# A memory layer and eight experts in one kernel: new wave order, stacked gated-bias product, last expert by pairs of tiles

## The reference, cut to what matters

```
x  = x + ln(memory(ln(x)))          # layer 1
x  = x + ln(experts(ln(x)))         # layer 2

memory(x):
  k, q, v = x@Wk+bk, x@Wq+bq, x@Wv+bv;  alr = 0.1*sigmoid(x@Wlr+blr)
  h1 = k + silu(k@W1+b1);  pred = h1 + silu(h1@W2+b2)
  loss = sum(alr * mean((pred - v)**2))      # gradients of W1, b1, W2, b2 over all tokens
  p_new = p*(1-1e-4) - 0.01*g/(sqrt(g*g)+1e-8)     # one Adam step of each
  return the same two layers with the new W1, b1, W2, b2, applied to q

experts(x):
  z = ln(x)*g + b;  p = softmax(z@rW + rb);  w = the two largest p, over their sum, 0 elsewhere
  y = sum over e of w[e] * (gelu(z@W1[e]+b1[e]) @ W2[e] + b2[e])    # 8 experts, hidden width 256
  return x + y
```

## Time and profile before

| | us |
|---|---|
| median of three runs | 206.26 |
| profiled execution | 204.86 |
| its span | 203.1 |
| PE busy | 178.0 (88%) |
| DVE busy | 145.4 (72%) |
| ACT busy | 99.1 (49%) |
| POOL busy | 22.1 (11%) |

### The profile page before, as it was taken

One profiled execution on the slowest core, in us unless ns is written; L12 is line 12 of the kernel. 1 busy time (PEld: TensorE's weight loads), 2 busy tenths in 40 slices (PEclk: granted clock), 3 DMA queues, 4 the chain that ended last, 5 costly groups with the idle time before them and its releaser, 6 DMA issues.

```text
span 203.1 us, 3196 instructions
## 1 busy us (share of the span) xinstructions
PE 178.0 (88%) x1089; PEld 140.8 (69%) x1089; DVE 145.4 (72%) x564; ACT 99.1 (49%) x150; POOL 22.1 (11%) x30
## 2 busy tenths in 40 slices
PE   7388988897988796999999999999999999999930
PEld 7334454465644484879999699988799897889920
DVE  0987695879685799979348977668976656475474
ACT  2157682946444309934567326384355495334200
POOL 1440000000000140032000131001211000010010
PEclk9999999999999999999999999999999999999996
DMA  5970000000000000000000000100000100001001
GB/s 153 342 233 4 0 0 3 0 0 0 0 3 2 0 2 0 3 0 0 3 0 2 0 3 0 52 3 0 2 0 3 52 0 3 2 2 52 3 0 52
DMA packets 3232, 4.96 MB, mean 24 GB/s; under 512 B 240, under 2 KB 1552, under 8 KB 3216
## 3 DMA queue, kind: packets, MB, share of 16 engines
q1 hardware_dynamic: 3216, 4.76, 7.2%
HBM read 3.71 MB, written 1.05 MB: 23 GB/s over the span
## 4 chain that ended last, share of the span: by engine, by line
PE 69%; DVE 17%; ACT 7%; issue 3%; DMA 2%; POOL 0%; POOLq 0%; DVEq 0%; ACTq 0%
PE bank L330 65%; DVE stats L737 3%; PE bank L338 2%; DMA x_tok<-in_x_dram 2%; ACT sig L580 2%; DVE xnT L1020 2%; ACT nsig L587 2%; DVE mv L740 1%; DVE s L870 1%; DVE s L878 1%; DVE xnT L874 1%; DVE vT L881 1%; ACT s L580 1%; ACT alrT L580 1%; ACT kT L576 1%
## 5 line engine op out<-in xcount | busy, mean ns | idle before, releaser
L1020 DVE SCALAR_TENSOR_TENSOR xnT<-bank,w_tok,xnT 128x128 f32<-128x128 f32 x128 | 36.0, 344 | 27.7 <-PE bank L330 27.3
L297 POOL TENSOR_TENSOR rstd<-vpe,minus_half 128x4 f32<-128x4 f32 (+1 forms) x21 | 20.7, 995 | 175.5 <-DVE vpe L745 162.0
L330 PE MATMUL bank<-z_hi,fW_hi 128*128 128x512 f32 x64 | 27.8, 435 | 1.5 <-DVE z_lo L915 1.5
L330 PE MATMUL bank<-z_lo,fW_hi 128*128 128x512 f32 x64 | 25.2, 394 | 0.0
L330 PE MATMUL bank<-z_hi,fW_lo 128*128 128x512 f32 x64 | 25.0, 390 | 0.0
L330 PEld LDWEIGHTS bank<-fW_sb,sig 128*128 128x128 f32 x192 | 22.8, 192 | 2.2 <-ACT h1T L686 1.5
L330 PE MATMUL bank<-fW_sb,sig 128*128 128x128 f32 x192 | 23.4, 276 | 0.0
L686 ACT ACTIVATE sig<-bank,early_sb 128x512 f32<-128x512 f32 x24 | 16.2, 688 | 13.8 <-PE bank L330 13.7
L686 ACT ACTIVATE k_tok<-bank,early_sb 128x512 f32<-128x512 f32 x20 | 13.5, 688 | 15.4 <-PE bank L330 15.3
L330 PEld LDWEIGHTS bank<-fW_sb,k_tok 128*128 128x128 f32 x160 | 19.3, 191 | 1.5 <-ACT sig L686 0.8
L330 PEld LDWEIGHTS bank<-fW_sb,h1T 128*128 128x128 f32 x160 | 19.3, 191 | 1.5 <-ACT k_tok L686 0.8
(11 more groups left out here) (129 smaller groups left out, 270.4 us busy)
## 6 DMA issues: line engine op xcount, KB each, us to landing
x_tok<-in_x_dram SPq DMA_DIRECT2D x4, 256.0 KB, 4.4
fW_raw<-in_fW_dram SPq DMA_DIRECT2D x1, 1024.0 KB, 9.2
out_dram<-xn_tok SPq DMA_DIRECT2D x3, 256.0 KB, 2.5
early_sb<-in_early_dram SPq DMA_DIRECT2D x1, 268.0 KB, 4.1
late_sb<-in_late_dram SPq DMA_DIRECT2D x1, 264.0 KB, 4.8
out_dram<-xn_tok SPq DMA_DIRECT2D x2, 128.0 KB, 2.0
b_diag<-in_late_dram SPq DMA_DIRECT2D x4, 4.0 KB
fW_sb<-in_fW_dram SPq DMA_DIRECT2D x1, 0.5 KB, 11.7
```

Of the source, the lines that this page charges most:

```text
L297: pool.tensor_tensor(rstd[:, ln, where], vpe[:, ln, where], minus_half[:, 0:where.stop - where.start], ALU.pow).then_inc(rstd_ready[ln], 1)
L330: return pe.matmul(out_, lhsT, rhs, start=start, stop=stop)
L1020: last = dve.scalar_tensor_tensor(out=y_tok[:, t, :], in0=bank[Y_BANK[m % len(Y_BANK)]][:, i * P:(i + 1) * P], scalar=w_tok[:, t, e:e + 1] ...
```

## The change

- `WAVE` and `LAG` are new. 1 - sigmoid is a step of its own (`n1`, `n2`), behind `h1` and behind `k`. `alr` now belongs to block w, not w + 1, and comes earlier; it leaves the prologue. `fw` begins a wave earlier (its first piece is in ACT's prologue) and DVE's `fw1_low(w)` is in wave w, the last piece behind the loop.
- Adam: the biases' sum comes first, and their chain is interleaved with W2's, not with W1's.
- Bias term: DVE writes four copies of the weights next to each other (high part twice, low part twice; 128 columns), in two more instructions at the end of `route`; they are transposed into 128 rows. `b2_diag` has 128 rows (high, low, high, low), so that one fp32r product gives the sum. It is filled by 16 small transfers, and POOL makes its rounded parts in three instructions of 512 columns, behind `rsqrt(L1, 0)`.
- Last expert: `output(31)` writes its first two tiles to bank 4 and the others to bank 7, and signals after each pair. DVE adds the first pair, takes its statistics, adds the second, takes its statistics, and then does the two `y_norm`.
- ACT subtracts the residual's mean from `x1_tok` (four instructions per block, slots 4, 12, 20, 28), so `y_norm` loses two small linked instructions.

```diff
-        WAVE = ["dh1", "dz2", "z2", "h1", "z1", "dz1", "gw2", "k", "gw1", "v", "alr", "x", "kp", "fw"]
-        LAG = {"dh1": -1, "dz2": -1, "z2": 0, "h1": 0, "z1": 1, "dz1": -1, "gw2": -1, "k": 0, "gw1": -1,
-               "v": 1, "alr": 1, "x": 3, "kp": 2, "fw": 0}
+        WAVE = ["dh1", "dz2", "z2", "h1", "n2", "z1", "alr", "gw2", "dz1", "v", "gw1", "k", "n1", "kp", "x", "fw"]
+        LAG = {"dh1": -1, "dz2": -1, "z2": 0, "h1": 0, "n2": 0, "z1": 1, "alr": 0, "gw2": -1, "dz1": -1,
+               "v": 1, "gw1": -1, "k": 0, "n1": 1, "kp": 2, "x": 3, "fw": 1}
...
-            for t in range(TB):
-                sp.dma_start(b2_diag[t * E:(t + 1) * E, t * H:(t + 1) * H],
+            for first in range(0, P, E):
+                t = first // E % TB
+                sp.dma_start(b2_raw[first:first + E, t * H:(t + 1) * H],
                              late[0:E, b2_first:b2_first + b2_width]).then_inc(b2_in, 16)
...
             rsqrt(L1, 0)
+            pool.wait_ge(b2_in, 16 * P // E)
+            pool.tensor_scalar(b2_diag[:], b2_raw[:], 1.0, 0.0, ALU.mult, ALU.add).then_inc(b2_high, 1)
+            pool.wait_ge(b2_high, 1)
+            for i, first in enumerate((TE, 3 * TE)):
+                rows = slice(first, first + TE)
+                pool.tensor_tensor(b2_diag[rows, :], b2_raw[rows, :], b2_diag[rows, :].bitcast(F32),
+                                   ALU.subtract).then_inc(b2_ready, 1)
+                pool.wait_ge(b2_ready, i + 1)
...
             def w_transpose(b):
-                pe.wait_ge(w_ready, b + 1)
+                pe.wait_ge(w_low, b + 1)
                 pe.wait_ge(zhi_done, b + 1)
-                pe.transpose(bank[7][0:TB * E, 0:P], w_tok[:, TB * b:TB * b + TB, :].rearrange("p t e -> p (t e)"),
-                             ident[:]).then_inc(w_tr, 1)
+                pe.transpose(bank[7][:, 0:P], w_parts[:, b, :].bitcast(F32), ident[:]).then_inc(w_tr, 1)
...
                 for i in range(TB):
+                    if m == STEPS - 1:
+                        into = bank[LAST_BANK[i // HALF]]
+                        if i == HALF:
+                            last.then_inc(y_mm, 1)
...
+            def centre_residual(b):
+                act.wait_ge(init_done, b + 1)
+                act.wait_ge(shift_ready, b + 1)
+                for t in tiles(b):
+                    last = act.activation(x1_tok[:, t, :], x1_tok[:, t, :], ACT.Identity, bias=neg_shift[:, t:t + 1])
+                last.then_inc(centred, 1)
...
-                if w:
-                    fw1_low(w - 1)
+                if w < NB - 1:
+                    fw1_low(w)
                 if w < NB:
                     layer2(w)
+            fw1_low(NB - 1)
             dve.wait_ge(late_in, 16)
             dve.wait_ge(gw2_mm, 1)
-            run(adam(w2n[:], w2_sb, bank[0][:, 0:P], adam_tmp[:, 0, :], adam_tmp[:, 1, :], w2n_ready))
             dve.wait_ge(dz1_done, NB)
             run(link(dve.tensor_reduce(gbs[:], gb[:], AX_X, ALU.add)))
+            run(adam(w2n[:], w2_sb, bank[0][:, 0:P], adam_tmp[:, 0, :], adam_tmp[:, 1, :], w2n_ready),
+                adam(bn[:], cols[:, B1:B1 + 2], gbs[:], gb_tmp[:], gb[:, 0, 0:2], bn_ready))
             dve.wait_ge(w2n_ready, 1)
             dve.wait_ge(gw1_mm, 1)
-            run(adam(w1n[:], w1_sb, bank[4][:, 0:P], adam_tmp[:, 0, :], adam_tmp[:, 1, :], w1n_ready),
-                adam(bn[:], cols[:, B1:B1 + 2], gbs[:], gb_tmp[:], gb[:, 0, 0:2], bn_ready))
+            run(adam(w1n[:], w1_sb, bank[4][:, 0:P], adam_tmp[:, 0, :], adam_tmp[:, 1, :], w1n_ready))
...
                 dve.tensor_tensor(tok(w_tok, b), p, first, ALU.mult).then_inc(w_ready, 1)
+                yield
+                dve.wait_ge(w_ready, b + 1)
+                weight = tok(w_tok, b).rearrange("p t e -> p (t e)").unsqueeze(1).to_broadcast([P, 2, TE])
+                parts = w_parts[:, b, :].rearrange("p (i c) -> p i c", c=TE)
+                dve.tensor_scalar(parts[:, 0:2, :], weight, 1.0, None, ALU.mult).then_inc(w_high, 1)
+                yield
+                dve.wait_ge(w_high, b + 1)
+                dve.tensor_tensor(parts[:, 2:4, :], weight, parts[:, 0:2, :].bitcast(F32),
+                                  ALU.subtract).then_inc(w_low, 1)
...
-            run(y_stats(NB - 1), y_stats(NB))
-            run(y_norm(NB - 1), y_norm(NB))
+            add_last_expert(0)
+            run(y_stats(NB - 1))
+            add_last_expert(1)
+            run(y_stats(NB))
+            run(y_norm(NB - 1))
+            run(y_norm(NB))
```

More of the change, by code:

```diff
@@ L141, in memory_and_experts @@
         rstd = sb("rstd", [P, 5, T])
-        shift = sb("shift", [P, 2, T])
+        neg_shift = sb("neg_shift", [P, T])
         minus_half = sb("minus_half", [P, TB])
@@ L156, in memory_and_experts @@
             "zeroed", "ident_ready", "half_ready", "table_ready", "ramp_ready"))
-        b2_zeroed, b2_in, fw_hi_done, fw_lo_done = (sem(n) for n in (
-            "b2_zeroed", "b2_in", "fw_hi_done", "fw_lo_done"))
+        b2_zeroed, b2_in, b2_high, b2_ready, fw_hi_done, fw_lo_done = (sem(n) for n in (
+            "b2_zeroed", "b2_in", "b2_high", "b2_ready", "fw_hi_done", "fw_lo_done"))
         dve_step = sem("dve_step")
@@ L225, in memory_and_experts @@
         H_BANK, Y_BANK, B2_BANK = (0, 1, 5), (6, 2), 3
+        LAST_BANK = (4, 7)
+        HALF = TB // 2
         AHEAD = 2
@@ L306, in _ @@
                       allow_small_or_imprecise_dtypes=True).then_inc(ramp_ready, 1)
-            pool.memset(b2_diag[:], 0.0).then_inc(b2_zeroed, 1)
+            pool.memset(b2_raw[:], 0.0).then_inc(b2_zeroed, 1)
             rsqrt(LR_, 0)
@@ L419, in _ @@
             k_product(1)
-            alr_product(0)
             feature_major_x(2)
@@ L667, in wT_out @@
                 act.wait_ge(w_tr, b + 1)
-                copy(wT[:, b * P:(b + 1) * P], bank[7][0:TB * E, 0:P], wT_ready)
+                copy(wT[:, b * P:(b + 1) * P], bank[7][:, 0:P], wT_ready)
             rsig1_out(0)
@@ L694, in _ @@
                     wT_out(0)
+                if slot >= 0 and slot % E == CENTRE:
+                    centre_residual(slot // E)
                 if due(Z_TR, slot):
@@ L897, in residual @@
                 last.then_inc(x1_ready, 1)
-                dve.tensor_tensor(shift[:, 0, span(b)], mv[:, LR_, span(b), 0], rstd[:, LR_, span(b)],
-                                  ALU.mult).then_inc(shift_ready, 1)
+                dve.scalar_tensor_tensor(out=neg_shift[:, span(b)], in0=mv[:, LR_, span(b), 0], scalar=-1.0,
+                                         in1=rstd[:, LR_, span(b)], op0=ALU.mult,
+                                         op1=ALU.mult).then_inc(shift_ready, 1)
                 yield
@@ L1024, in add_expert, with add_last_expert @@
                 last.then_inc(acc_done, 1)
+            def add_last_expert(half):
+                dve.wait_ge(y_mm, STEPS + half)
+                dve.wait_ge(acc_done, STEPS - 1)
+                for i in range(half * HALF, half * HALF + HALF):
+                    t = T - TB + i
+                    last = dve.scalar_tensor_tensor(out=y_tok[:, t, :],
+                                                    in0=bank[LAST_BANK[half]][:, i * P:(i + 1) * P],
+                                                    scalar=w_tok[:, t, E - 1:E], in1=y_tok[:, t, :],
+                                                    op0=ALU.mult, op1=ALU.add)
+                last.then_inc(acc_done, 1)
             def y_stats(q):
                 first, count = PARTS[q]
-                dve.wait_ge(acc_done, (first // TB + 1) * E)
+                dve.wait_ge(acc_done, (first // TB + 1) * E + (1 if q == NB else 0))
                 yield from statistics(LY, range(first, first + count), lambda i, t: y_tok[:, t, :])
@@ L1037, in y_norm @@
                 dve.wait_ge(rstd_ready[LY], q + 1)
[L1038 to L1041, removed]
-                yield from link(dve.tensor_tensor(shift[:, 1, where], shift[:, 1, where],
-                                                  shift[:, 0, where], ALU.subtract))
+                dve.wait_ge(centred, where.start // TB + 1)
                 for t in range(where.start, where.stop):
-                    last = dve.tensor_scalar(y_tok[:, t, :], y_tok[:, t, :], rstd[:, LY, t:t + 1],
-                                             shift[:, 1, t:t + 1], ALU.mult, ALU.add)
+                    last = dve.tensor_scalar(y_tok[:, t, :], y_tok[:, t, :], mv[:, LY, t, 0:1],
+                                             rstd[:, LY, t:t + 1], ALU.subtract, ALU.mult)
                 yield from link(last)
@@ L1068, in _ @@
                         start_sum(slot // E)
-                    add_expert(slot)
+                    if slot < STEPS - 1:
+                        add_expert(slot)
                 if due(NORM_R, slot):
```

29 lines of the change are left out of this document (18 added, 11 removed).

## The result

The changed kernel takes 196.88 us (median of four runs, 196.28 to 197.03) against 206.24 us (the three runs of before and a fourth, 204.58); the ratio is 0.958 with a 95% interval of 0.954 to 0.962. The ratio leaves slow runs out and is not the quotient of the two medians, which is 0.955. The forecast was 198.6 us, with a range of 196.4 to 201.2. The profiled executions differ by 8.1 us (204.86 and 196.74), their spans by 8.5. The remaining 1.2 us of the 9.4 are in the medians: that of before lies 1.4 above its profile, as was said, that of the changed kernel 0.1 above its own. The sum is therefore judged by the spans. Part of this level goes with PE's clock: of the runs of the kernel before that stand beside the experiments, 33 enter the ratios and have their span and mean granted clock on record.

A forecast was written before the change was run, and what follows sets the result against it. PE was taken to bound the experts' part, step order the first stage. First stage -5.9, Adam 0, POOL +1.2, experts -1.2, end -1.75 make -7.65; from 206.26 that gives 198.6 us, range 196.4 to 201.2.

The forecast's parts named there:

- rival 1: Retrieval, before the first hidden product: POOL's b2 instructions do not disturb DVE; -8.85, 197.4 us; chance 25%.
- a walk 0.6 better than mine: First stage: the step-by-step timing of the waves, which gave -5.9, improved by 0.6 for the range's low end.
- First stage, -5.9: Waves up to dh1(3): with the waits gone PE bounds a full wave at 8.9 us; dh1(3) at 46.2, not 52.13.
- Adam, 0: Adam's new order changes nothing, since its end stays covered by PE's work, with 0.8 us of cover left.
- POOL, +1.2: Retrieval: one of POOL's three b2 instructions, at 1.1 us, stands fully in DVE's way; +1.2 us.
- Bias term, -0.85: Experts' part: one fp32r product for the bias term gains 0.85 us per block, -2.55 for blocks 1 to 3.
- The two waits of +0.5: At w_transpose of blocks 1 and 2, PE waits 0.5 us longer each for the end of the routing.
- Block 0, +0.27: At output(2), PE waits for expert 0's sum, 0.5 us later on DVE; +0.27 instead of -0.85.
- End, -1.75: After the last product: last expert by pairs, fewer small linked steps; additions end 1.75 us earlier, last transfer moves with them.
- the third: First stage: the waves do not close up, only the waits visible in the rows go (-3.3); 201.2 us; chance 10%.
- the fourth: POOL's elementwise work costs what its rsqrt does, 80 us per instruction; slower than before; chance 2%.
- the second: The lock decides every meeting for POOL, holding DVE's two-input instructions twice; +2.1 instead of +1.2, 199.5 us; chance 20%.

The follow-up runs named there:

- e1: The kernel before with the new wave order alone (1 - sigmoid split off, alr moved, W1 pieces a wave earlier): 199.9 us, ratio 0.971.
- e5: The kernel before in its old wave order, with only the 1 - sigmoid steps moved behind h1 and behind k: 203.14 us, ratio 0.990.
- e6: The kernel before with the new order of the other steps, 1 - sigmoid still directly behind its sigmoid: 200.45 us, ratio 0.976.
- e4: The changed kernel with Adam in the old order (biases beside W1): 196.75 us, ratio 0.961.
- e9: The changed kernel with POOL's three b2 instructions behind a wait for the new W1: 196.16 us, ratio 0.957.
- e10: The changed kernel with memsets in place of POOL's two subtractions, low part of b2 left out: 195.79 us in a single run.
- e7: The changed kernel with POOL's three b2 instructions moved ahead of the first rsqrt of the retrieval: 196.62 us, ratio 0.957.
- e2: The kernel before with the stacked gated-bias product alone (its POOL, PE and DVE parts): 204.73 us, ratio 0.998.
- e3: The kernel before with the last expert by pairs of tiles alone, y_norm as before: 204.86 us, ratio 0.997.
- e11: e9 with the weights' transpose of blocks 1 to 3 half a slot later, between two hidden products: 194.65 us, ratio 0.951.
- e12: e11 with block 0's two weight instructions behind norm_r(1), its transpose behind output(0), and ten clock-keeping transposes: 194.9 us, ratio 0.948.

## Why the prediction was right

The forecast of 198.6 us was too high by 1.7, and the mechanism is to be judged by the stretches, not by the total: 196.88 us is nearer to rival 1's 197.4 than to the forecast, yet POOL's rows refute rival 1. It also lies only 0.5 above the low end of the range, and that end rested on a walk 0.6 better than mine, beyond the -6.2 that the prediction itself gave as about the end. That the sum comes within 0.9 of the spans' -8.5 is in part luck, as two terms below show.

- **First stage, -5.9:** -6.06 once the load's 0.36 is taken out. That PE bounds a full wave at 8.9 was right (8.99). e1 shows the part alone; e5 and e6 show that inside the waves the order does it. My weighing of ACT's chain against the queue ahead of `dh1` was left open in the prediction: either alone shortens the waves (1.6 and 3.6 us), but they do not add (3.6 together).
- **Adam, 0:** right (e4).
- **POOL, +1.2:** right in cause (e9, e10) and, up to the first hidden product, in size (+1.15). It was the forecast's least certain term, taken from one stretched POOL row. It was split otherwise than I had it: not one hold, but one of 1.0 and one of 0.3. And the forecast carried it in full to `output(2)`, where only 0.84 of it arrives (e9 against e4).
- **Bias term, -0.85:** too small. It is 1.02: 0.92 up to the output, so the 0.07 that I had allowed for unprefetched weights was not there, and 0.10 behind it. Three times 0.17 are 0.5 of the 0.6 us that the stretch to the last product came out better than forecast. The two waits of +0.5 were right (0.53); block 3's +0.1 was 0.
- **Block 0, +0.27:** +0.55 was measured, but by another mechanism: PE was late by its clock, and DVE's sum was there in time. Where the clock was full and POOL out of the way (e7, e9) it is +0.35, with the predicted wait of PE for DVE (1.24 in e9). From `dh1(3)` to `output(2)` the measured +1.70 is thus 0.84 of POOL, 0.35 of DVE's longer chain and 0.52 of the clock, where the forecast had 1.2 + 0.27. That the two figures are close is luck.
- **End, -1.75:** right in sum (-1.73), by luck, and wrong in its shares: 0.9 for the pairs, 0.8 for ACT's subtraction. The additions gain 1.37, not 1.75; the last transfer, which was only to move with them, brings the other 0.36.
- Of the rivals, the first (POOL disturbs nothing) falls with the stretched rows, the third with the waves' lengths, the fourth with 1.26 us for 512 columns; the second had the mechanism, but only the first meeting cost a whole instruction.
- The **clock** had no place in the prediction. By the profiles it cost 0.5 here and 1.6 in e1.
- What made the forecast too high was the size of two terms (0.5 in the bias term, 0.5 in the first stage with the load) and, for over 1 us, the level of before's median.

## What to carry over

Where one in-order engine feeds a loop through two others, list what stands ahead of the loop's own step in its queue, and compare the loop's length with the engine's own work: their larger one is the new period, and the second shortening of the same slack gives nothing. Preparatory work on GpSimd that reads SBUF was free here only where it met no VectorE instruction with two SBUF inputs (e9), and work that only writes was free even beside one (e10); so ask what it reads and whom it meets, not only when GpSimd idles. When a step is added at the end of a chain for which PE waits, look for a place half a slot later for PE's step: here that gave back 1.33 us, where the two waits had grown by 1.06.

## What I had not expected of the hardware

The granted clock fell to half for one stretch in eight of the fourteen profiles, at one of two places: at the first hidden products in the changed kernel, e1 and e2, in the prologue in e3, e6, e9, e11 and e12. The other six have it nowhere ahead of the end, e4 among them, which differs from the changed kernel in nothing but Adam's order. Idle time ahead of it does not decide it alone: 1.49 us of it with a fall (e1) and without (before), 2.65 with (the changed kernel) and without (e4). In the prologue it shows in the page's slices, here those of e11:

```profile
PEclk9969999999999999999999999999999999999997
```

It costs 1.6 us at the experts unless PE would wait anyway, and about 1.15 in the prologue: from PE's first product of 512 columns to `dh1(0)` it takes 12.78 to 12.84 us with it (e9, e11, e12) and 11.64 to 11.67 in the same order without it (the changed kernel, e1, e4, e10). PE had waited 0.78 us ahead of that product in all of these. What sets it off was not settled. It is likely to be a part of the spread between runs of one kernel, because the runs of before with the longer spans are those with the lower mean clock (section on the result); no experiment held the clock and looked at the spread.
